# Row selection by matmul in a graph network kernel: a wider selection, and target rows spread by DMA

## What is computed

```python
def _bn(x, g, b):
    mu = jnp.mean(x, axis=0)
    var = jnp.mean((x - mu) ** 2, axis=0)
    return g * (x - mu) * jax.lax.rsqrt(var + EPS) + b
x_src = h[src]
x_dst = h[dst]
e = (x_dst - x_src) @ theta_w.T + x_src @ phi_w.T
e = jax.nn.relu(_bn(e, bn0_g, bn0_b))
e = e @ fc1_w.T
e = jax.nn.relu(_bn(e, bn1_g, bn1_b))
agg = jax.ops.segment_sum(e, dst, num_segments=n)
cnt = jax.ops.segment_sum(jnp.ones((e.shape[0],), e.dtype), dst, num_segments=n)
x = agg / jnp.maximum(cnt, 1.0)[:, None]
return jax.nn.relu(x + h)
```

## Time and profile before

| what | value |
|---|---|
| median of 3 runs | 2537.24 us (2537.05 to 2538.57) |
| the profiled execution | 2537.5 us |
| its span, first to last instruction | 2535.7 us |
| mean granted TensorE clock | 0.888 |
| PE busy | 2051.7 us (81%) |
| DVE busy | 1546.1 us (61%) |
| POOL busy | 1562.5 us (62%) |
| ACT busy | 652.8 us (26%) |
| second pass, first to last gather | 1037.59 to 1957.63 us |

### The profile page before, as it was taken

The page is one execution under the profiler, slowest core; times in us unless marked ns, Lnnn a source line. Parts: engine busy times, 40 slices in busy tenths (PEclk is TensorE's granted clock), DMA queues, the critical chain, the costliest instruction groups (busy, mean ns, idle before and its releaser), DMA issues. The chain is left out here.

```text
span 2535.7 us, 49004 instructions
## 1 busy us (share of the span) xinstructions
PE 2051.7 (81%) x13488; PEld 1691.6 (67%) x13489; DVE 1546.1 (61%) x4106; ACT 652.8 (26%) x1087; POOL 1562.5 (62%) x1715
## 2 busy tenths in 40 slices
PE   4777777777677677689888888988988998999996
PEld 3766666666667667546666666666665444999995
DVE  5443433434433344787867767777776787777776
ACT  3211111111111112541111111111111774444444
POOL 6777777777777775477777777777777001940002
PEclk9988888888888888759889989988988999999998
DMA  4222222222222221553434333343343993344442
GB/s 108 73 65 72 70 67 72 64 72 64 74 71 64 71 60 41 175 177 116 134 114 134 115 124 125 115 133 117 114 134 111 329 303 129 131 141 146 146 149 84
DMA packets 129354, 291.65 MB, mean 115 GB/s; under 512 B 34541, under 2 KB 83478, under 8 KB 111492
## 3 DMA queue, kind: packets, MB, share of 16 engines
q1 hardware_dynamic: 72532, 139.41, 17.1%
q0 software_dynamic: 48640, 99.61, 15.2%
q10 hardware_dynamic: 8112, 51.91, 5.2%
HBM read 227.59 MB, written 63.21 MB: 115 GB/s over the span
## 5 line engine op out<-in xcount | busy, mean ns | idle before, releaser
L759 POOL DMA_INDIRECT G<-in_x,srcT x782 | 744.3, 952 | 246.2 <-issue 180.4
L774 POOL DMA_INDIRECT G<-btab,srcT x738 | 696.3, 943 | 268.9 <-issue 167.6
L858 PE MATMUL PS<-BIG,G 128*128 128x192 f32 x1564 | 354.6, 379 | 258.6 <-PEq L36 257.6
L858 PEld LDWEIGHTS PS<-BIG,G 128*128 128x128 f32 x1564 | 297.2, 220 | 289.9 <-issue 289.4
L1145 ACT ACTIVATE BIG<-PS 128x768 f32<-128x768 f32 x196 | 158.5, 809 | 785.0 <-ACTq L36 784.6
L1460 DVE TENSOR_TENSOR ACC<-ACC,PS 128x24 f32 x782 | 140.8, 180 | 318.6 <-DVEq L36 228.1
L869 PE MATMUL PS<-BIG 128*128 128x192 f32 (+1 forms) x1584 | 329.5, 370 | 0.5 <-PEq L36 0.5
L869 PEld LDWEIGHTS PS<-BIG 128*128 128x128 f32 x1584 | 318.5, 227 | 0.6 <-issue 0.6
L987 PE MATMUL PS<-BIG,ACC 128*128 128x256 bf16 x2112 | 286.9, 297 | 24.8 <-PEq L36 24.7
L987 PEld LDWEIGHTS PS<-BIG,ACC 128*128 128x128 bf16 x2112 | 215.3, 106 | 96.1 <-issue 54.9
L1234 ACT ACTIVATE BIG<-PS 128x512 f32<-128x512 f32 x174 | 103.7, 596 | 594.4 <-ACTq L36 588.8
(11 more groups left out here) (208 smaller groups left out, 2347.6 us busy)
## 6 DMA issues: line engine op xcount, KB each, us to landing
BIG<-spill SPq DMA_DIRECT2D x90, 1024.0 KB, 4.9
spill<-BIG ACTq DMA_DIRECT2D x49, 1024.0 KB
G<-in_x,srcT POOLq DMA_INDIRECT x782
typ_i<-in_edge_type SPq DMA_DIRECT2D x97, 128.0 KB
G<-btab,srcT POOLq DMA_INDIRECT x738
BIG<-atab SPq DMA_DIRECT2D x196, 60.0 KB
atab<-BIG SPq DMA_DIRECT2D x12, 384.0 KB, 2.9
xn<-in_x SPq DMA_DIRECT2D x48, 64.0 KB
```

The lines of the kernel that those rows point to most:

```text
L759: nc.gpsimd.indirect_dma_start(out=G[0:n, g % 2, t, :], out_offset=None, in_=x, in_offset=bass.IndirectOffsetOnAxis(ap=srcT[0:n, TPG * g + ...
L774: nc.gpsimd.indirect_dma_start(out=G[0:n, g % 2, t, :], out_offset=None, in_=btab[:, :], in_offset=bass.IndirectOffsetOnAxis(ap=srcT[0:n, ...
L858: mm = pe.matmul(PS[:, 2 * c + q // 2, (q % 2) * ZW:(q % 2 + 1) * ZW], G[:, h, TPC * k + q, :], soh[:, p, TPC * c + q, :, :].rearrange("p ...
```

## The change

The diff does four things.

1. **Three tiles selected in place of two, from pair 1 on.** `PICK` is 384 edges, `PICK_Q` 1. The selection products and one-hots have 384 columns. There are ten batches of 5 windows (the last has 4 real ones) in place of seven of 7. They stand behind chunks 0 (one), 1 (two), 2 (one), 3 (two), 4 (one), 5 (two) and 6 (one). ACT writes five codes, one for each window of a batch (with the bias lowered by j), so that one DVE instruction makes the five one-hots of a batch: 15 rows of 128 elements at a step of 130. PE's `spread_picks` now stands ahead of chunk 0's products, and ACT's `code_picks` ahead of its copy of chunk 0.
2. **The table two units a chunk.** Two PSUM banks take turns, and 13 units are made in the first 7 chunks. The load buffers stay two.
3. **The targets as one row.** The setup writes the relative targets of each chunk as a bf16 row (three pieces of 171 at a step of 172) to `rel_d`, and as float32 to `relf_d` for windows beyond the first. SP loads a group's row, repeated on 80 partitions (80 x 4128 bytes), in place of the digits, and DVE makes `ohT` straight from it. PE's spreading products, `digits` and `d_ready` are gone.
4. **A PSUM bank for each of four chunks.** A chunk's e stands in bank k, not 2 + k % 2, and `e_free` starts at four. At chunk 7 ACT copies 128 and 384 columns with two instructions.

The core of the diff:

```diff
-    PICK = 2 * TILE
-    PICK_Q = TPC - 2
-    FIRST_PICK = 2
-    PICK_ROW, PICK_COLS, PICK_STEP = 3, 86, 88
-    BATCH = 7
+    PICK = 3 * TILE
+    PICK_Q = TPC - 3
+    FIRST_PICK = 1
+    PICK_ROW, PICK_COLS, PICK_STEP = 3, TILE, TILE + 2
+    BATCH = 5
+    NBATCH = 10
     ACC_UNITS = 8
+    REL_ROW, REL_COLS = 3, 171
+    REL_STEP = REL_COLS + 1
+    REL_CHUNK = REL_ROW * REL_STEP
...
+        rel = BIG[0:WIN, at[0] - CPG * REL_CHUNK:at[0]].bitcast(BF16).rearrange("p (s k n) -> p s k n", s=2, k=CPG)
...
-            return {1: (0,), 2: (1,), 3: (2,), 4: (3,), 5: (4,), 6: (5, 6)}.get(at_c, ())
+            return {0: (0,), 1: (1, 2), 2: (3,), 3: (4, 5), 4: (6,), 5: (7, 8), 6: (9,)}.get(at_c, ())
...
-        def unit_of(g, k):
-
-            return CPG * g + k if isinstance(g, int) and CPG * g + k < NBU else None
+        def units_of(g, k):
+
+            return range(2 * (CPG * g + k), min(2 * (CPG * g + k) + 2, NBU)) if isinstance(g, int) else ()
 
         def unit_bank(u):
-            return PS[:, 5, 0:len(real_windows(u)) * D].rearrange("p (w d) -> p w d", d=D)
+            return PS[:, 4 + u % 2, 0:len(real_windows(u)) * D].rearrange("p (w d) -> p w d", d=D)
...
             def load_digits(g, h):
                 take(sp, dig_free)
-                sp.dma_start(digits[:, h, :], digits_d[:, bass.ds(g * GROUP, GROUP)]).then_inc(dig_in[h], 16)
+                row = rel_d[bass.ds(g * CPG, CPG), :].rearrange("(o k) n -> o (k n)", o=1).to_broadcast([WIN, CPG * REL_CHUNK])
+                sp.dma_start(rel[:, h, :, :].rearrange("p k n -> p (k n)"), row).then_inc(dig_in[h], 16)
...
+                            sp.dma_start(relx, relf_d[bass.ds(CPG * g + k, 1), :].to_broadcast([WIN, CHUNK])).then_inc(relx_in, 16)
                         if wide_chunks:
                             further_windows(sp, reach, further)
-                        u = unit_of(g, k)
-                        if u is not None and u >= 2:
-                            load_unit(u)
-                        if isinstance(g, int) and (g, k) == (2 * FIRST_PICK - 1, 0):
+                        for u in units_of(g, k):
+                            if u >= 2:
+                                load_unit(u)
+                        if isinstance(g, int) and (g, k) == (2 * FIRST_PICK - 1, 1):
...
-            def spread_dst(g, h, use, k):
-                if k == 0:
-                    reached(pe, "pe", dig_in[h], 16 * (use + 1))
-                pe.matmul(PS[:, k % 2, :], onesb[0:2, :], digits[:, h, k * CHUNK:(k + 1) * CHUNK],
-                          start=True, stop=True).then_inc(d_ready, 1)
...
-                for w in range(BATCH * b, BATCH * (b + 1)):
+                for w in range(BATCH * b, min(BATCH * (b + 1), NW)):
                     for a in range(3):
-                        mm = pe.matmul(picked, table_part(w, a), pick_oh[:, BATCH * (b % 2) + w % BATCH, 0:PICK],
+                        mm = pe.matmul(picked, table_part(w, a), pick_oh[:, BATCH * (b % 2) + w % BATCH, :],
                                        start=(w == 0 and a == 0), stop=False, skip_group_check=True)
                 mm.then_inc(pick_oh_free, 1)
...
+                    return (PS[:, k, 0:CHUNK - PICK], slice(0, CHUNK - PICK)), (picked, slice(CHUNK - PICK, CHUNK))
+                return ((PS[:, k, :], slice(0, CHUNK)),)
...
+                        if picking(g, h, use) and h == 0 and k == 0:
+                            spread_picks()
                         reached(pe, "pe", b_gathered[CPG * h + k], b_landed(g, h, use, k))
                         take(pe, e_free)
                         for q in (range(PICK_Q) if picks(g, h, use, k) else range(TPC)):
-                            pe.matmul(PS[:, 2 + k % 2, q * TILE:(q + 1) * TILE], G[:, h, TPC * k + q, :], ident[:, :],
+                            pe.matmul(PS[:, k, q * TILE:(q + 1) * TILE], G[:, h, TPC * k + q, :], ident[:, :],
...
-                        nxt = after(g, h, use, k)
-                        nxt = nxt and after(*nxt)
-                        if nxt:
-                            spread_dst(*nxt)
                         if isinstance(g, int) and (g, k) == (2 * FIRST_PICK - 1, CPG - 1):
                             pe.wait_ge(tab_ready, NBU)
-                        if picking(g, h, use) and h == 0 and k == 0:
-                            spread_picks()
                         for b in picked_batches(g, h, use, k):
                             pick_rows_of(b)
...
-                if u >= 1:
-                    act.wait_ge(tab_ready, u)
+                if u >= 2:
+                    act.wait_ge(tab_ready, u - 1)
...
             def code_picks():
                 take(act, pick_spread_done)
                 act.sem_inc(pick_rows_free, 1)
-                full = PICK // PICK_COLS
-                act.activation(pick_code[:, 0:full, 0:PICK_COLS], pick_spread[:, 0:full * PICK_COLS].rearrange("p (r c) -> p r c", r=full),
-                               ACT.Identity, bias=small[:, 62:63])
-                act.activation(pick_code[:, full, 0:PICK - full * PICK_COLS], pick_spread[:, full * PICK_COLS:PICK],
-                               ACT.Identity, bias=small[:, 62:63]).then_inc(pick_code_ready, 1)
+                for j in range(BATCH):
+                    ins = act.activation(pick_code[:, j, :, 0:PICK_COLS], pick_spread.rearrange("p (r c) -> p r c", r=PICK_ROW),
+                                         ACT.Identity, bias=pick_bias[:, j:j + 1])
+                ins.then_inc(pick_code_ready, 1)
...
-                    u = unit_of(g, k)
-                    if u is not None:
+                    for u in units_of(g, k):
                         unit_high_part(u)
+                    if picking(g, h, use) and h == 0 and k == 0:
+                        code_picks()
                     take(act, look_done)
                     act.sem_inc(g_free, 1)
                     act.sem_inc(aw_free, 1)
                     to = stage[:, stage_of(g, h), k * CHUNK:(k + 1) * CHUNK]
                     if picks(g, h, use, k):
-                        act.activation(to.rearrange("p (a n) -> p a n", a=2), PS[:, 2 + k % 2:4 + k % 2, 0:PICK], ACT.Copy).then_inc(act_self, 1)
+                        act.activation(to[:, 0:CHUNK - PICK], PS[:, k, 0:CHUNK - PICK], ACT.Copy)
+                        act.activation(to[:, CHUNK - PICK:CHUNK], picked, ACT.Copy).then_inc(act_self, 1)
                         take(act, act_self)
                         act.sem_inc(pick_copied, 1)
                         act.sem_inc(tab_read, 1)
                     else:
-                        act.activation(to, PS[:, 2 + k % 2, :], ACT.Copy).then_inc(act_self, 1)
+                        act.activation(to, PS[:, k, :], ACT.Copy).then_inc(act_self, 1)
                         take(act, act_self)
                     act.sem_inc(e_free, 1)
                     act.sem_inc(e_copied, 1)
-                    if u is not None:
+                    for u in units_of(g, k):
                         unit_mid_part(u)
-                    if picking(g, h, use) and h == 0 and k == 0:
-                        code_picks()
...
+            f_chunks = f_rel.rearrange("p (c t) e -> p c (t e)", **in_chunks)
+            step(dve.memset(rel_rows_b, -1.0))
+            step(dve.tensor_copy(rel_rows_b[:, :, 0:2, 0:REL_COLS], f_chunks[:, :, 0:2 * REL_COLS].rearrange("p c (r n) -> p c r n", r=2)))
+            step(dve.tensor_copy(rel_rows_b[:, :, 2, 0:CHUNK - 2 * REL_COLS], f_chunks[:, :, 2 * REL_COLS:CHUNK]))
...
-            def look_up(k):
-                take(dve, d_ready)
-                dve.tensor_scalar(ohT[0:WIN, k % 2, :], PS[0:WIN, k % 2, :], node_col[0:WIN, 0:1], None, ALU.is_equal).then_inc(ohT_ready, 1)
+            def look_up(g, h, use, k):
+                if k == 0:
+                    reached(dve, "dve", dig_in[h], 16 * (use + 1))
+                dve.tensor_scalar(ohT[0:WIN, k % 2, 0:CHUNK + 1].rearrange("p (r n) -> p r n", r=REL_ROW),
+                                  rel[:, h, k, :].rearrange("p (r n) -> p r n", r=REL_ROW)[:, :, 0:REL_COLS],
+                                  node_col[0:WIN, 0:1], None, ALU.is_equal).then_inc(ohT_ready, 1)
...
+                for j in range(BATCH):
+                    step(dve.tensor_scalar(pick_bias[:, j:j + 1], node_col[:, 0:1], -64.0, -float(j), ALU.mult, ALU.add))
                 dve.sem_inc(picks_ready, 1)
-                step(dve.tensor_scalar(small[:, 62:63], node_col[:, 0:1], -64.0, None, ALU.mult))
-                step(dve.memset(pick_code[:, :, :], -1.0))
                 dve.sem_inc(pick_oh_free, 2)
 
             def pick_hots(b):
                 if b == 0:
                     take(dve, pick_code_ready)
-                    take(dve, pick_oh_free, 2)
-                    dve.sem_inc(pick_oh_free, 1)
-                else:
-                    take(dve, pick_oh_free)
-                for w in range(BATCH * b, BATCH * (b + 1)):
```

(25 more changed lines are left out.)

47 lines of the change are left out of this document (22 added, 25 removed).

## The result

The changed kernel takes **2641.99 us** (median of 5 runs, 2641.03 to 2647.93), the kernel before 2537.24 us: 1.0419 times as long, with a 95% interval from 1.0404 to 1.0433. The profiled execution took 2641.03 us, its span is 2639.1 us: 103.4 us more than the 2535.7 of before. The prediction said 2657 us, slower.

The account below looks back on a forecast made before the run. The bound moves from POOL's gathers to a ring through PE, ACT and DVE: 33.2 + 6.3 = 39.5 us, plus 2.6 for the clock, 42.1 a pair. 2537.5 + 127 - 7 = 2657 us, range 2590 to 2700.

Parts of the forecast that it names:

- The ring: Loop from a pair's first batch through ACT's copy of chunk 7 to the next first batch: 39.5 us, above POOL's 36.2.
- part two: ACT's copy of chunk 7 to PE's first batch: two copies, gap, five codings, one-hots; 6.3 us, ends 5.0 and 7.5.
- Part one: PE work from the first batch to ACT's copy of chunk 7: 147 products, six fronts, chunk 7; 33.2 us.
- The clock: PE's granted clock falls in its wait at the seam, slowing work behind it: 2.6 us a pair, between 0 and 3.4.
- DVE itself is free by then: DVE's other seam work ends 3.4 us behind the copy's end, before the codings, which need 4.2 us.
- Chunk 7's copy: First pair's last copy, with two table units a chunk and two load buffers: at 1110 us, range 1099 to 1122.
- The end: From the last copy to the next pass: four fronts and 4.4 us, 11 us in place of 18, -7.
- the unrolled ones: Four pairs are unrolled and save the loop's branch: 2 us off 23 pairs of 42.1 us.
- Rival 1: PE's clock holds through the shorter gap, ring 39.5 us, 60 us lower: 2597 us; chance 0.15.
- Rival 2: POOL stays the bound: 2506 us, if copy to first batch takes 3.0 us or less; chance 0.05.
- Rival 3: DVE's one-hots run at one element a cycle, ring 1 us longer: 2680 us, up to 2700; chance 0.10.
- What I had costed at nothing: Look-up from SBUF, target rows on SP's queue, the setup's conversions and its two larger stores: no cost counted.

Follow-up runs that it names:

- e3: Changed kernel with four of the five codings left out, so four of five windows select by stale codes: 2606.52 us, 1.0265 of before.
- e4: Changed kernel with 36 unused products of 256 columns put between chunk 0's front and the first batch on PE: 2598.6 us, 1.023 of before.
- e5: e1 with the first batch's one-hots made on DVE ahead of the statistics of chunk 7: 2575.01 us, 1.0143 of before.
- e2: Changed kernel with only the batch schedule altered: two batches each in chunks 2 to 6, none in chunks 0 and 1: 2644.75 us, 1.0418 of before.
- e1: Changed kernel with spread and codings moved one chunk earlier, into chunk 7 of the pair before: 2646.63 us, 1.042 of before.
- e6: e5 with the spread ahead of the last batch's products in chunk 6 and the codings behind ACT's copy of chunk 6: 2565.55 us, 1.0101 of before.
- e7: e6 with the table split one unit a chunk and selection from the third pair on: 2532.07 us, 0.9978 of before.
- e11: e7 with the batches' one-hots ahead of the next chunk's look-up on DVE: 2509.49 us, 0.9892 of before.
- e9: Changed kernel with two tiles selected instead of three and the code stored as one row of 256 a window: 2544.97 us, 1.0029 of before.
- e10: Changed kernel with the code in six rows of 64 a window instead of three of 128, 30 source rows a batch: 2643.18 us, 1.0414 of before.

## Why the prediction was right

**The ring.** The step that carried the forecast, that PE can do nothing behind chunk 0's front until the first one-hots exist, holds, and e3, e4 and e5 show it from three sides. Term by term: part two 6.3 us, measured 6.45 (codings 2.46 against 2.50, gap 1.76 against 1.70, one-hots 1.15 against 1.14). Part one 33.2 us, measured warm 32.2: the next copy of chunk 7 comes 34.5 us after the first batch, less 2.3 for the clock. This term was mis-sized. I took a front as 1.39 us up to the end of its count products, but PE's next batch starts 1.20 us after the transposes (1413.98 to 1415.18, and so in each chunk). Seven times 0.19 is 1.3 us, less 0.3 for products at 0.162 and not 0.160. The clock was put at 2.6 us; the batch shows 2.3, and the pairs of e4, in which the clock holds, take 38.7 us: the other two terms, 32.2 + 6.45. Together 32.2 + 6.45 + 2.3 = 40.95 us a pair, not 42.1.

**The DVE leg.** "DVE itself is free by then", 3.4 us behind the copy's end against the codings' 4.2: right for the sum (DVE idles 1.25 us ahead of the one-hots), but I did not see what it meant. The ring has two legs of nearly one length, and in e2 a third, SP's load of chunk 2's window, comes to light: cutting one of them alone was worth little or nothing (e1, e2, part of e3), and of that little the clock took its share. I had also put the target rows on SP's queue at nothing; they stay hidden in the changed kernel, but e2 shows what waits behind them.

**Start and end.** Chunk 7's copy was put at 1110 us (1099 to 1122); it came at 1116.6. Chunk 0 was copied 1.7 us earlier than before, at 1071.9, but the next six chunks took 7.05 us each and not 5.6 (one of them 10.8), and the last 2.4. ACT waited 1.3 to 2.7 us for the load of one of the two units in nearly every chunk. The end was priced at 11 us and took 14.05: the last chunk's look-up stood on DVE behind statistics and a copy of the moments that waited, a step that I had left out.

**The sum** reads, as measured: 1116.6 + 23 x 40.92 = 2057.7, then -4.1 and -0.8 against the copy at 1949.4. The 16 us between 2657 and the profiled 2641 are 27 too many in the pairs, of which 2 were taken off for the unrolled ones, 7 too few in the table phase and 2 too few at the end. The errors are of opposite sign, so part of the closeness is luck; the pairs alone were 25 us too long.

**The rivals.** Rival 1 (the clock holds) was priced at 2597; e4, where it is made to hold, gives 2598.6 (the pairs 38.7 us, where the rival had 39.5). Unaided it fell in every seam of the changed kernel looked at, and behind waits of 1.8 us in 12 of 17 seams of e6 and 8 of 17 of e7. Rival 2, POOL as the bound at 2506, needed a part two of 3.0 us; e11, whose seam allows it, takes 2509.5 with 716 gathers. Rival 3 did not come: 15 rows of 128 take 1.146 us for 1920 elements, as forecast. What I had costed at nothing (target rows by DMA, the setup) stayed small, as e9 shows: all of it together with the new table phase comes to 1.0029 of before, 7 us, where POOL waits 10.4 us in the table phase and has two gathers fewer.

## What to carry to other kernels

A resource whose work fits into the bound's shadow can still become the bound by order: follow the dependences once around the loop, through every engine that works in order, and price the ring as well as each engine's sum. When one leg is cut and nothing moves, look for the leg beside it before giving up the ring, a DMA queue's among them, and look whether the clock gives the shorter wait back as slower work; on each engine, issue first what the waiting engine needs first. And a faster form of an instruction is to be judged by the neighbour that shares its port.

## What was unexpected

- **Idle work that pays.** 36 useless products in each pair made the kernel 43.4 us faster: the granted clock is 1.00 over the pairs, where it was 0.92.
- **Short waits can be enough, and the same waits not always.** Two waits of 0.75 and 1.8 us close together (e6) were followed by a granted clock of 0.5 in 12 of 17 seams and by 1.00 in the other five. With 0.75 and 0.5 us (e11) the clock stayed at 1.00 but for the pairs in which PE waited for a gather.
- **Different seams, one time.** The changed kernel, e1, e2 and e10 wait 4.4 to 5.5 us a pair in different places, and all take 41.0 us a pair.
- **DVE against POOL.** With an even number of source rows the one-hots took 0.48 us for 1280 elements and lengthened many of the gathers that met them, 943 to 992 ns in the mean of 736. The other way round, 41 of the 230 fast one-hot instructions of e10 took 0.88 to 0.91 us instead of 0.65; each of them began some 0.5 us into a gather.
